# Second step's score tiles and short exponential moved behind the first step's, value products behind the expert's down product

## The reference

```python
# attention: 16 heads of 16, ALiBi slopes, causal; per head
scores = q @ k.T * SCALE + (j - i) * slope[h]        # 1024 x 1024, -inf above the diagonal
attn   = max(softmax(scores), 1e-10)
att    = attn @ v
s      = concat(att) @ out_w.T + out_b
# mixture: 2048 tokens, 32 experts, 4 chosen for each, at most 128 places in one
x      = rmsnorm(xn) * w_norm;  w, sel = top_k(softmax(x @ w_router), 4)
y[e]   = (silu(buf[e] @ w_gate[e]) * (buf[e] @ w_up[e])) @ w_down[e]     # buf[e]: the expert's 128 rows
f      = xn + sum over the chosen of w * y + sigmoid(x @ w_sg) * ((silu(x @ sw_gate) * (x @ sw_up)) @ sw_down)
```

## Time and profile before

| | us |
|---|---|
| three runs, median | 661.56 |
| lowest and highest | 656.74, 702.24 |
| the profiled execution, its span | 661.1 |
| TensorE busy in it | 577.8 |
| VectorE, ScalarE, GpSimd busy | 469.4, 454.4, 264.7 |

### The profile page before, as it was taken

One profiled execution on the slowest core, in us unless ns is written; L12 is line 12 of the kernel. 1 busy time (PEld: TensorE's weight loads), 2 busy tenths in 40 slices (PEclk: granted clock), 3 DMA queues, 4 the chain that ended last, 5 costly groups with the idle time before them and its releaser, 6 DMA issues.

```text
span 661.1 us, 17857 instructions
## 1 busy us (share of the span) xinstructions
PE 577.8 (87%) x4903; PEld 423.8 (64%) x4904; DVE 469.4 (71%) x1038; ACT 454.4 (69%) x1049; POOL 264.7 (40%) x628
## 2 busy tenths in 40 slices
PE   1698578789988999999999999999998999999575
PEld 1694237566766766766777667766776777667354
DVE  5988955476677767776777777677767766777247
ACT  2321664367787778888888888788888888888350
POOL 7620000233553445445544554454445455543200
PEclk9859879697999999999999999999999999999798
DMA  8990366532334334334434343344335433421374
GB/s 252 165 267 32 104 175 185 150 87 63 87 85 104 82 92 95 88 86 109 98 87 89 82 98 94 89 88 99 88 89 105 101 85 82 72 50 21 105 251 175
DMA packets 80658, 72.01 MB, mean 109 GB/s; under 512 B 18098, under 2 KB 71028, under 8 KB 80628
## 3 DMA queue, kind: packets, MB, share of 16 engines
q1 hardware_dynamic: 72580, 60.91, 33.8%
q0 software_dynamic: 8048, 10.75, 10.7%
HBM read 48.34 MB, written 23.07 MB: 108 GB/s over the span
## 4 chain that ended last, share of the span: by engine, by line
PE 59%; ACT 13%; issue 8%; DVE 8%; DMA 6%; SPq 3%; ACTq 1%; POOL 0%; DVEq 0%; POOLq 0%
PE PSB L822 8%; PE PSB L760 8%; PE PSB L861 7%; PE PSB L734 6%; PE PSB L782 5%; ACT PB L1012 5%; ACT PSB L1003 5%; PE PSB L832 4%; PE PSB L779 4%; PE PSB L756 4%; PE PSB L853 3%; PE PSB L730 3%; DMA STACKS<-CT 2%; PE PSB L883 2%; PE PSB L635 2%
## 5 line engine op out<-in xcount | busy, mean ns | idle before, releaser
L1263 DVE TENSOR_REDUCE NEGM<-PSB 128x1 f32<-128x1024 f32 (+7 forms) x256 | 192.1, 751 | 71.2 <-PE PSB L734 60.9
L1003 ACT ACTIVATE PSB<-PSB,NEGM 128x1024 f32<-128x1024 f32 (+7 forms) x256 | 183.5, 717 | 30.9 <-DVE NEGM L1263 30.8
L1012 ACT ACTIVATE PB<-PSB 128x128 f32<-128x128 f32 (+7 forms) x256 | 166.6, 653 | 54.8 <-PE PSB L760 43.1
L1269 DVE TENSOR_SCALAR PB<-PB 128x128 f32<-128x128 f32 (+7 forms) x256 | 114.8, 458 | 50.3 <-ACT PB L1012 47.5
L734 PE MATMUL PSB<-STACKS 111*128 111x512 bf16 (+3 forms) x384 | 107.5, 335 | 0.0
L760 PE MATMUL PSB<-STACKS 111*128 111x512 bf16 (+3 forms) x384 | 104.7, 327 | 0.0
L756 PE MATMUL PSB<-MK,IDB 128*128 128x128 bf16 x256 | 57.3, 224 | 29.2 <-ACT PSB L1003 16.2
L779 PE MATMUL PSB<-PB,VH 128*32 128x256 f32 x640 | 69.0, 387 | 0.0
L756 PEld LDWEIGHTS PSB<-MK,IDB 128*128 128x128 bf16 x256 | 24.7, 97 | 63.7 <-ACT PB L1012 29.0
L1555 POOL DMA_INDIRECT moe_rows<-YE,IDX x32 | 53.8, 1680 | 29.5 <-issue 29.5
L1515 POOL COPY IDX<-TABS 128x2 int32 (+1 forms) x32 | 27.9, 871 | 80.1 <-DVE VS L1254 80.1
(11 more groups left out here) (193 smaller groups left out, 1225.1 us busy)
## 6 DMA issues: line engine op xcount, KB each, us to landing
STACKS<-q_parts SPq DMA_DIRECT2D x192, 32.0 KB, 1.8
STACKS<-k_parts SPq DMA_DIRECT2D x192, 32.0 KB, 1.8
WG<-in_L_ffn_w_gate_dram SPq DMA_DIRECT2D x32, 176.0 KB
WU<-in_L_ffn_w_up_dram SPq DMA_DIRECT2D x32, 176.0 KB
WDS<-in_L_ffn_w_down_dram SPq DMA_DIRECT2D x32, 176.0 KB
q_parts<-PB SPq DMA_DIRECT2D x8, 384.0 KB, 2.6
XN<-in_L_attn_qkv_dram SPq DMA_DIRECT2D x4, 512.0 KB, 5.8
moe_rows<-XN SPq DMA_DIRECT2D x1, 2048.0 KB, 8.7
```

Of the source, the lines that this page charges most:

```text
L1003: act.activation(sc, sc, ACT.Exp, bias=NEGM[:, par, i:i + 1], accum_out=LSUM[:, par, i:i + 1]).then_inc(exp1_done, 1)
L1012: act.activation(PB[:, k % 2, prob_offset(s):prob_offset(s) + (s + 1) * P], psf[:, base:base + (s + 1) * P], ACT.Exp).then_inc(exp2_done, 1)
L1263: dve.tensor_reduce(NEGM[:, par, i:i + 1], psf[:, base:base + (i + 1) * P], AX_X, ALU.max, negate=True).then_inc(max_ready, 1)
L1269: dve.tensor_scalar(p, p, FLOOR, 0.0, ALU.subtract, ALU.max).then_inc(clamp_done, 1)
```

## The change

In step 0 of a phase ScalarE now takes `exp2(k, 0)` and `exp2(k, 1)`, one behind the other, and only then `exp1(k + 2, 0)`. On TensorE `values(k - 1, 0)` leaves step 0 and runs in step 1 behind the expert's down product and ahead of the turn `TR`; with it gone, the tiles of step 1 of both passes follow those of step 0 directly. On VectorE `row_max(k + 2, 1)` follows `row_max(k + 2, 0)` directly; `silu_up` of `SB`, `clamp(k - 1, 7)` and `clamp(k, 0)` come behind both. GpSimd's and SyncE's lists, and all waits written in the functions, stay as they are.

```diff
@@ TensorE, phase
                         pass2(it, k, s, exists(it, k + 2))
-                    if s == 0 and exists(it, k - 1):
-                        values(it, k - 1, 0)
                     if s == 1 and exists(it, w - 1):
                         expert_down(it, w - 1, *aux_begin(it, w - 1, DN))
+                    if s == 1 and exists(it, k - 1):
+                        values(it, k - 1, 0)
                     if s == 1 and exists(it, w):
                         expert_transpose(it, w, *aux_begin(it, w, TR))
@@ ScalarE, phase
-                    if exists(it, k):
+                    if s != 1 and exists(it, k):
                         exp2(it, k, s, exists(it, k + 2))
+                    if s == 0 and exists(it, k):
+                        exp2(it, k, 1, exists(it, k + 2))
@@ VectorE, phase
-                    if s > 0 and exists(it, k):
+                    if s > 1 and exists(it, k):
                         clamp(it, k, s - 1)
                     if exists(it, k + 2):
                         row_max(it, k + 2, s)
-                    if s == 0 and exists(it, w - 1):
+                    if s == 1 and exists(it, w - 1):
                         shared(it, w - 1, SB)
-                    if s == 0 and exists(it, k - 1):
+                    if s == 1 and exists(it, k - 1):
                         clamp(it, k - 1, NQ - 1)
+                    if s == 1 and exists(it, k):
+                        clamp(it, k, 0)
```

## The result

The kernel with the change took 664.67 us in the median of ten runs (661.45 to 666.19), the kernel before 659.42 beside it on the same chip. The ratio is 1.0078, 95% interval [1.0054, 1.0101]. A second measurement gave 664.15 us and 1.0071 [1.0046, 1.0097]. The forecast was 3.8 us less than before; it came out about 5 us more. (The three runs of before that the forecast started from had a median of 661.56; ten runs put it at 659.42.) That is within 2% either way, but it has the other sign. One of the ten runs before took 702.24 us in a slow state of the chip, and the ratios are taken without such runs.

What follows compares the result with a forecast made beforehand. TensorE's own work was taken to set the pace, apart from a 0.7 us wait in three phases of four; 661.1 - 2.9 (steady) + 0.8 (start) - 1.7 (end) = 657.3, median 657.8 us; own range 653 to 664, 8-in-10 range 647 to 667.

Steps and rivals of the forecast that it cites:

- What TensorE gains: Step 4, three phases in four: row maximum and exponential start sooner behind step 3's first-pass tile, 0.17 to 0.18 us gained.
- The rule that the prediction weighed: Steady gap can mean too few buffers; then no reordering removes step 4's wait, and the steady part's sum would be zero.
- the bubble: Step 4, three phases in four: TensorE's second pass idles some 0.7 us until an exponential frees bank 3.
- the same before and after, only in another order: TensorE's work ahead of step 3's first-pass tile: unchanged apart from order, so that tile is complete at 341.83.
- pass2(1)'s wait: Step 1, TensorE waits for exp2(k, 0): 0.05 to 0.1 us in phases 12 and 13, nothing in 14 and 15.
- nothing in the steady part: Rival: the new wait for exp2(k, 0) eats the 0.17 us gain; only start and end count, 660.7 us; chance 0.22.
- The earlier chain buys nothing: Steady part, GpSimd and SyncE: work released up to 1.6 us sooner gains nothing, as TensorE's position times the shift's turn.
- New waits for the turn: TR in the loop: HS ends at 338.65, TensorE reaches TR at 339.02, 0.4 us to spare, no cost.
- the slower rival: HS ends later than TensorE reaches TR, 0.75 us in 22 phases, +16.5 us, 675.9 us in all; chance 0.06.
- The start: Phase -1: second row maximum ahead of HS lengthens the turn's 0.80 us wait; +0.8 us, bounds 0.3 and 1.1.
- The end: Phase 30: the chain from down product to the shift's turn starts 1.6 to 1.7 us earlier; -1.7 us, bounds -1.2 and -1.9.
- three signs that would have shown the forecast wrong: L807 waits in the loop; the wait at step 4 is gone; value products take longer than 1.6 us when moved.

Runs made afterwards that it cites:

- a_values_first: Kernel after, with the value products ahead of the down product, still in step 1; 667.58 us, ratio 1.0098.
- b_tensor_only: Kernel before, with only TensorE's part of the change (value products behind the down product); 664.22 us, ratio 1.0063.
- d_no_tensor: Kernel before, with only ScalarE's and VectorE's part of the change, TensorE in its old order; 689.88 us, ratio 1.0444.
- e_turn_first: Kernel after, with the turn ahead of the value products and the gather not held; 687.87 us, ratio 1.0452.
- g_weigh_behind: Kernel before, with exp1(k + 2, 1) ahead of weigh and exp_seed on ScalarE; 669.22 us, ratio 1.0151.
- c_gather_late: Kernel after, with GpSimd's gather held until step 7's score tiles; 660.35 us, ratio 0.9976; repeated, 659.85 us, 1.0004.
- after_again: Kernel after, unaltered, measured a second time against the kernel before; 664.15 us, ratio 1.0071.
- l_end_only: Kernel before, with the value products behind the down product in phase 30 alone; 658.44 us, ratio 0.9976.

## Why the prediction was wrong

**What TensorE gains (predicted 0.17 to 0.18 us a phase in three phases of four): right.** The third column fell by 0.20, 0.21 and 0.21, phase 13 nothing. The cause, the down product's earlier place with ScalarE's list hanging on it, is shown by a_values_first and b_tensor_only. d_no_tensor, e_turn_first and g_weigh_behind, where the stretch is longer by a wait or ScalarE's order is turned, have the same gain. The rule that the prediction weighed (the Trainium skill, Perfetto Trace Analysis, section Optimization Strategy) gives the bubble to bank 3; 1.8 of its 2.2 us are still there, so the trace agrees.

**The sentence that failed: TensorE's list from pass1(0) to pass1(3) is "the same before and after, only in another order".** The work is the same and the list took 1.03 us more in four phases: 0.43 us for pass2(1)'s wait, where the prediction had 0.12 (0.07 and 0.05) and took none in phases 14 and 15; 0.40 for the down product and 0.20 for the turn, where it had nothing. Its own bound, 0.2 us in each phase, was for the wait alone. It also placed pass1(1) at 335.9, while its link puts it 0.126 us behind pass2(0), at 335.78 in the times of before, so that pass2(1) reaches its wait 0.1 us sooner. The sum of the two parts was therefore 1.03 - 0.62 = +0.4 us in four phases, where the forecast had -0.40, and this is what c_gather_late, with the gather out of the way, shows (61.49 against 61.09; over the five groups from phase 8 to 27, 307.22 against 305.34). The rival "nothing in the steady part" had named this list and its growth, and had priced it as high as the gain and no higher.

**"The earlier chain buys nothing" on GpSimd and SyncE: it cost.** The prediction named the queues that the step releases sooner and priced them at zero because nobody waits for them. It didn't ask what they meet. The gather moved onto the shift's transfers: +0.28 us in four phases in this order (0.7 in phases 12 to 15 of after_again), 0.9 in b_tensor_only (first column). Removing it gave 2.5 to 3.0 us between phases 2 and 26 (372.50 and 372.49 with it, 369.54 to 369.96 in the four profiles without).

**What the four phases did not stand for.** Prediction and ledger both take phases 12 to 15 for all 29. Phases 4 and 6 of the kernel before are not like them: pass2(0) comes 1.44 and 1.26 us behind the first tile (1.13 and 1.29 in l_end_only), waiting for the shift. In front of phase 6 the gather is issued 1.35 us behind the turn, and its packets and the third transfer's move until 4.50 and 4.52 us behind it (3.95 and 3.83 in front of phase 10, where nothing is lost); in front of phase 4 it is issued at 2.56, as in g. With the change and the gather held they are 0.67 and 0.56. So the old order has the collision too, early in the loop, and phases 4 to 7 are shorter with the change (62.34 against 62.77 us, and 61.52 with the gather held).

**New waits for the turn: right.** HS ended where it was worked out, and the slower rival didn't happen. d_no_tensor and e_turn_first show how near it was: without the value products in front, 1.0 to 1.2 us of wait.

**The start: right in kind, smaller.** Predicted +0.8, bounds 0.3 and 1.1. The profile after, phase -1, beside the earlier trace rows:

```profile
135.55 2.22 DVE L1265 TENSOR_REDUCE NEGM<-PSB 128x1 f32<-128x1024 f32 x2 [1.10 <-PE PSB L734]
...
138.14 0.42 DVE L1293 SCALAR_TENSOR_TENSOR HS<-RT,PSB 128x256 f32<-128x256 f32 x1
...
138.61 0.44 PE L807 MATMUL PSB<-IDF,XES 128*128 128x128 f32 x2 [1.79 <-DVE HS L1293]
```

The wait grew from 0.80 to 1.79 (predicted about 1.8); the phase grew from 10.48 to 10.94 us, so half was taken back.

**The end: right, -1.7 predicted, -1.6 measured.** Phase 30 after, beside the earlier trace rows:

```profile
612.41 1.03 PE L832 MATMUL PSB<-WDS,HE 88*128 88x256 f32 x4
...
613.85 0.20 ACT L1018 ACTIVATE LEX<-LNS 128x8 f32<-128x8 f32 x1
...
618.98 0.28 PE L801 MATMUL PSB<-IDB,C 128*24 128x128 bf16 x1 [1.28 <-POOL C L1486]
```

**The sum, with the measured terms:** from phase 2 to pass2(30, 0) the change takes 434.83 us against 429.98, +4.9 (0.68 x 7.25 is the same); the start +0.5, the end -1.6, in all +3.8 us. Measured were +4.7 to +5.3, each with an interval of about 1.6 us to either side. The rest is not explained. With the gather held (c) the stretch is 431.24, +1.3. The start is as above, and the end gives 1.6 to 2.0 us (the turn of the shift comes 6.50 us behind pass2(30, 0) in c, 6.87 in the change, 8.47 before), so the sum is within 0.2 us of nothing: level, as measured.

**The range.** The forecast's own range, 653 to 664 us, does not follow from the bounds given. Added up (-3.8 to +5.8, +0.3 to +1.1, -1.9 to -1.2, and 0.5 for the runs) they give 656 to 667 us, and 664.67 lies in that: in the upper part, which the prediction had for a wait of 0.2 us in every phase without any gain. The wait was smaller, 0.07 to 0.14, and the gain came, so the number in that range is not the mechanism's merit. Of the three signs that would have shown the forecast wrong none came (no wait of L807 in the loop, the wait at step 4 still there, the value products at 1.463 us first to last as before); what gave it away were the lengths of the phases, 15.23 and 16.76 us against 14.7 to 14.9 and 16.5.

**The down product and the turn, and what stays open.** The down product's four matmuls take 0.723 instead of 0.649 us and the turn's two 0.165 instead of 0.113. It is the same 0.72 in every kernel that has the values moved behind it, whether pass2(1) waited 0.07 or 0.14 us ahead of it. Nearly all of it lies in the first link, from the first matmul to the second (0.291 instead of 0.219 in the down product; the others are 0.215 to 0.216 in both). The weight loads in the traces say more: the first one hides less behind the task ahead. From the down product's first weight load to its last matmul it is 0.76 us before, and 0.75 in the change and in a_values_first. What differs is how far that load starts ahead of the first matmul: 0.110 us before, 0.031 in the change, 0.002 in a, where the four take 0.752. The turn's first load starts 0.214 us ahead of its matmul behind the down product, and 0.002 to 0.031 behind the values or behind a wait. Why the load starts later in those places is not shown; I had no experiment that changes only this.

## What to carry to other kernels

When a task is moved to relieve a bubble, price TensorE's list again link by link, start to start, and not only by the durations of its tasks: here four small links cost more than the bubble gave. Look at how far each task's first weight load stands ahead of its first matmul; a task that is moved can lose that lead. For every queue that the move releases sooner, ask which small, urgent transfer its data will meet, with the time to landing and not with the span shown for the instruction. And look for the one place where the move can't hurt: in phase 30 alone the traces keep the whole 1.6 us, and in the loop it lost more. Compare the first phases of a loop with its steady ones before multiplying.

## What the runs showed of the hardware

An indirect gather of GpSimd delays small transfers when its data move, 1.8 to 2.2 us behind its issue, and not while it is issued: with the turn as zero, pass2(0) came 0.2 to 0.5 us late when the gather was issued at 0.50 to 0.83, 0.7 to 0.9 late at 1.47, and at its usual time when the gather was issued at 0.48 or earlier or at 2.28 to 2.35. The Trainium skill, DMA: Bandwidth & Descriptors, section SWDGE vs HWDGE vs iDMA, says that the two kinds feed different queues inside each DMA engine, which takes them in turn; by that rule a small transfer beside a gather is late and not blocked. The trace agrees: in front of phase 12 the shift's delayed packets begin at 332.30, while the gather's last until 332.67.

The end of the program differs by a microsecond from one execution to the next. The stretch from the last L801 to the last head's evacuation, of the kernel before, of the two profiles of the same kernel after, and of c_gather_late (columns as above):

```profile
618.97:638.64 19.67, 15.98 (x159) 11.14 (x160) 6.07 (x13) 9.30 (x15) 2.00 (x2) 0.83 0.87 272
```

```profile
618.98:639.36 20.38, 17.64 (x159) 11.61 (x160) 6.23 (x14) 9.59 (x15) 2.27 (x2) 0.75 0.84 263
```

```profile
619.91:639.18 19.27, 15.77 (x159) 11.24 (x160) 6.08 (x13) 9.29 (x15) 2.00 (x2) 0.82 0.87 274
```

```profile
615.82:636.40 20.58, 16.89 (x159) 11.53 (x160) 6.17 (x13) 9.52 (x16) 2.00 (x2) 0.83 0.85 264
```

The same code took 20.38 us at a mean granted clock of 0.75 and 19.27 at 0.82. The clock is not all of it: at 0.83 the stretch took 19.67 us in one kernel and 20.58 in another. A difference of a microsecond at the end of one profile is not to be put down to the change.
